# A graph network's count matrix: own products in fp32, evicted behind the third eviction of counts

## The reference

```python
def _layer(x, rows, cols, vals, W, b):
    neigh = segment_sum(vals[:, None] * x[cols], rows, num_segments=N)
    cat = concatenate([x, neigh], axis=1)
    return relu(cat @ W.T + b)
x0 = _layer(_layer(x, src, dst, 1/deg, W0, b0), src, dst, 1/deg, W1, b1)
x = layernorm(x + x0)
h_neigh = x @ W_neigh
summed = segment_sum(maxk(h_neigh, 32)[src], dst, num_segments=n)
x = layernorm(x + x @ W_self + summed / max(deg_in, 1)[:, None])
```

## Time and profile before

| what | us |
|---|---|
| median of the 3 timed runs | 697.11 |
| the three runs | 697.01, 697.11, 700.86 |
| the profiled execution | 701.42 |
| its span, first to last instruction | 699.6 |
| TensorE busy in it | 641.8 |
| VectorE busy | 505.9 |
| ScalarE busy | 348.7 |
| GpSimd busy | 106.9 |

### The profile page before, as it was taken

How to read it: one execution, slowest core, us unless ns; L and a number is a source line. 1 busy time by engine, 2 the same in 40 slices (tenths; PEclk the granted TensorE clock), 3 DMA queues, 4 the chain that set the end, 5 groups by cost and what they waited for, 6 DMA issues and landing times.

```text
span 699.6 us, 11372 instructions
## 1 busy us (share of the span) xinstructions
PE 641.8 (92%) x4012; PEld 338.4 (48%) x4013; DVE 505.9 (72%) x1296; ACT 348.7 (50%) x669; POOL 106.9 (15%) x188
## 2 busy tenths in 40 slices
PE   8867788888787999999999999999999889999996
PEld 3355566666643444444444444444444334444443
DVE  8659989999768788888883578787877844634433
ACT  3588888899847777777774223333333220100000
POOL 3001222222111001010100222323232210000000
PEclk9789999999998999999999999999999999999999
DMA  9423554555531011111111555555656414310000
GB/s 212 91 91 113 188 162 137 162 161 158 157 101 37 29 43 33 41 34 40 36 40 39 156 174 164 172 167 169 176 162 182 121 36 135 115 47 23 22 28 25
DMA packets 39542, 73.08 MB, mean 104 GB/s; under 512 B 3120, under 2 KB 32207, under 8 KB 39481
## 3 DMA queue, kind: packets, MB, share of 16 engines
q1 hardware_dynamic: 39481, 72.30, 34.8%
HBM read 38.91 MB, written 33.38 MB: 103 GB/s over the span
## 4 chain that ended last, share of the span: by engine, by line
PE 72%; DVE 17%; ACT 7%; issue 2%; DMA 2%; POOL 0%; SPq 0%; ACTq 0%; DVEq 0%; POOLq 0%
PE pair L1567 36%; PE bank L1679 9%; PE pair L1679 8%; PE bank L1467 7%; DVE hots L639 6%; PE pair L1467 4%; PE bank L1459 2%; DVE ct L782 2%; ACT own L1128 2%; DVE x_t L775 2%; PE bank L1473 1%; PE pair L1363 1%; DMA own_in<-own_dram 1%; ACT x_t L1121 1%; ACT slab L1078 1%
## 5 line engine op out<-in xcount | busy, mean ns | idle before, releaser
L1567 PE MATMUL pair<-xs,ct 125*128 125x512 f16 x625 | 144.1, 381 | 0.0
L1567 PE MATMUL pair<-a,ct 125*128 125x512 f16 x625 | 142.8, 379 | 0.0
L639 DVE TENSOR_TENSOR hots<-iota,jobs 125x1792 f16<-125x1792 f16 (+1 forms) x100 | 104.5, 1063 | 1.3 <-PE pair L1380 0.7
L1567 PEld LDWEIGHTS pair<-xs,ct 125*128 125x128 f16 x625 | 61.3, 100 | 68.7 <-issue 1.8
L1567 PEld LDWEIGHTS pair<-a,ct 125*128 125x128 f16 x625 | 61.0, 99 | 68.1
L1078 ACT ACTIVATE slab<-pair 125x875 f16<-125x875 f32 (+1 forms) x100 | 83.4, 858 | 5.6 <-PE pair L1380 4.1
L1245 ACT ACTIVATE a<-ct 125x1000 f16<-125x1000 f16 (+1 forms) x75 | 80.2, 1069 | 0.9
L1679 PE MATMUL bank<-xs,ct 125*128 125x512 f16 (+1 forms) x325 | 71.5, 379 | 0.0
L1679 PE MATMUL pair<-xs,ct 125*128 125x512 f16 x300 | 66.4, 379 | 0.0
L1459 PE MATMUL bank<-ident,slab 125*128 125x125 f16 x625 | 52.7, 224 | 14.0 <-DVE ct L782 9.9
L1318 ACT ACTIVATE sd<-mv,epsb 125x1 f32<-125x1 f32 x25 | 7.4, 294 | 113.9 <-DVE mv L998 113.9
(11 more groups left out here) (213 smaller groups left out, 852.9 us busy)
## 6 DMA issues: line engine op xcount, KB each, us to landing
c_dram<-slab SPq DMA_DIRECT2D x25, 683.6 KB
ct<-c_dram SPq DMA_DIRECT2D x25, 683.6 KB
own_in<-own_dram SPq DMA_DIRECT2D x50, 125.0 KB
own_dram<-own SPq DMA_DIRECT2D x25, 125.0 KB
own_dram<-own_st SPq DMA_DIRECT2D x25, 125.0 KB
x_in<-in_x_dram SPq DMA_DIRECT2D x25, 125.0 KB
z_dram<-z_st SPq DMA_DIRECT2D x25, 125.0 KB
a<-z_dram SPq DMA_DIRECT2D x5, 625.0 KB
```

The source lines that it names most:

```text
L639: v.tensor_tensor(hots[k][:, :, :, :].rearrange("p w g (a d) -> p (w g) a d", d=2), iota, job, ALU.is_equal).then_inc(win_hot, 1)
L1567: ins = mm(agg[k % 3][0:lhs.shape[1], :], lhs, parts[l][:, t, :], start=t == 0, stop=t == NT - 1, skip_group_check=True)
```

## The change

- An own product is two fp32 instructions (one per half, 512 columns each) on the fp32 transposed block and the fp32 transposed W0, where it was six fp16 matmuls. `own_low` and the split of W0 are gone: four weight halves are split (tiles 3 and 4), not six.
- The own eviction and the eviction of x_t stand behind ScalarE's third eviction of counts and ahead of its eviction of transposes of group 2; they stood ahead of the third eviction of counts.
- `OWN` starts in tile 3 and takes two products in tiles 8, 13 and 18.
- The statistics: the three squares of x in ScalarE's stream write their sums into `stat`, and a step on VectorE takes the root as a power of two from the bits. The fourth block of x and the weights are bounded by their largest magnitude on VectorE (tile 1). The roots and their table load are gone. The bounds move to tile 2 on TensorE and VectorE.
- In the second set of picks one warm matmul follows each of the 8 groups of three; `KEEP` loses its entry for tile 2.

```diff
-OWN = {0: [], 1: [], 2: [], 3: [], 4: [0], 5: [1], 6: [2], 7: [3, 4], 8: [5], 9: [6, 7], 10: [8], 11: [9, 10], 12: [11],
-       13: [12, 13], **{t: [t] for t in range(14, NT)}}
+TWOS = (8, 13, 18)
+OWN = {t: [] for t in range(3)}
+for _t in range(3, NT):
+    _n = sum(map(len, OWN.values()))
+    OWN[_t] = [_n, _n + 1] if _t in TWOS else [_n]
-KEEP = {0: 4, 1: 2, 2: 1}
+KEEP = {0: 4, 1: 2}
...
+            def largest_x(c):
+                dve.wait_ge(x_loaded[c], BOTH)
+                v.tensor_reduce(stat[0:P, c:c + 1], xs32[:, XC[c]:XC[c + 1], :].rearrange("p t f -> p (t f)"), X, ALU.max,
+                                apply_absolute_value=True).then_inc(stat_ready, 1)
+
+            def largest_w():
+                dve.wait_ge(b_loaded, 16)
+                v.tensor_reduce(stat[:, 14:16], bcol[:, :].rearrange("p (h o) -> p h o", o=1), X, ALU.max,
+                                apply_absolute_value=True).then_inc(stat_ready, 1)
...
+                step(v.tensor_scalar(sv[:, 0, 0:3].bitcast(I32), sv[:, 0, 0:3].bitcast(I32), 0.5, float((127 << 22) + (16 << 23)),
+                                     ALU.mult, ALU.add))
...
-            def own_low(t):
-
-                dve.wait_ge(own_tcopied, t + 1)
-                v.scalar_tensor_tensor(x_t16[:, 2:4, 0:P], xp, scales[:, 0:1], x_t16[:, 0:2, 0:P], ALU.mult, ALU.subtract
-                                       ).then_inc(own_tlo, 1)
...
-                a.activation(x_t16[:, 0:2, 0:P], xp, ACT.Copy, scale=scales[:, 0:1]).then_inc(own_tcopied, 1)
+                a.activation(x_t32[:, :, :], xp, ACT.Copy).then_inc(own_tcopied, 1)
...
                     quick_copy(t, 0)
-                    tr_copy(t - 1, 0)
...
-                        w_high(0)
-                        w_high(1)
+                    tr_copy(t - 1, 0)
+                    quick_copy(t, 1)
+                    if 2 < t < 5:
+                        w_high(2 * t - 6)
+                    quick_copy(t, 2)
                     if own:
                         own_copy(own[0], own[0] % 2, own[0] // 2)
-                    if t == 3:
+                    if t == 2:
                         own_t(0)
                     if own and own[0] + 1 < NT:
                         own_t(own[0] + 1)
-                    quick_copy(t, 2)
                     tr_copy(t - 1, 2)
-                    if t == 1:
-                        roots()
+                    if 2 < t < 5:
+                        w_high(2 * t - 5)
                     quick_copy(t, 3)
...
+                        if k:
+                            keep_clock(bank[7], 1)
                 last.then_inc(picked, 1)
+                if k == 0:
+                    pe.wait_ge(wt_copied, 2)
...
                 if h == 0:
-                    pe.wait_ge(own_tlo, t + 1)
+                    pe.wait_ge(own_tcopied, t + 1)
                     pe.wait_ge(own_copied, t + 1)
-                    pe.wait_ge(w_split, 2)
-                last = in_parts(bank[6][0:P, :], lambda k: x_t16[:, k, 0:P], w0_parts, (h,))
+                    pe.wait_ge(wt_copied, 2)
+                last = mm(bank[6][0:P, :].rearrange("p (a f) -> p a f", a=2), x_t32[:, h, :], w0_t[:, h::2, :], start=h == 0, stop=h == 1,
+                          skip_group_check=True)
...
                     fill(t, 0)
-                    if t == 3:
-                        scales_b()
+                    if t == 2:
+                        bounds_t()
...
                     transposes(t - 1, par, 0)
+                    fill(t, 1)
                     if t == 2:
-                        bounds_t()
-                    fill(t, 1)
+                        bounds_row()
...
                     transposes(t - 1, par, 2)
                     if t == 2:
-                        bounds_row()
+                        scales_b()
```

112 lines of the change are left out of this document (44 added, 68 removed).

## The result

| | before | after |
|---|---|---|
| median of the runs | 697.14 us (697.01, 697.11, 697.18, 700.86) | 709.07 us (706.84, 708.96, 709.17, 709.23) |
| profiled execution, its span | 701.42, 699.6 | 706.84, 705.0 |
| first transposes of tile 3, of tile 24 | 55.28, 186.02 | 54.17, 193.97 |
| first aggregation of the layers | 193.47 | 201.34 |

The ratio of the times is 1.0162, 95% interval 1.0131 to 1.0193: the changed kernel is 12 us slower. The forecast was 701.7 with a range up to 707.0, so it is wrong by 7.4 us and the time lies outside the range.

The account below looks back on a forecast made before the run. The loop through the slab was to replace VectorE as the bound of the count-matrix build. From 697.1: +4.2 stage, +0.7 start, -0.1 last tile, -0.2 picks gives 701.7 us; range 693.5 to 707.0.

Parts of the forecast that it names:

- loop of 5.76: Plain tile of the count-matrix build: loop through the slab takes 5.76 us, against 5.67 before; VectorE and ScalarE have slack.
- own half 0.86: TensorE's fp32 own half of 512 columns, taken as two matmul records of 0.43 us each.
- rival B: Own product: the fp32 half costs 0.43 us, a plain tile 5.33; time 688.4 us; chance 0.12.
- rival D: Plain tiles: links overlap more and a tile runs at VectorE's 5.2 us; time 692.7 us; chance 0.08.
- +0.7: Start of the stage, up to tile 3's transposes: new chain of scales costs +0.7 us, between -1 and +2.5.
- -2.0: Second picks: warm matmuls bring the clock back near 19.5 us; last pick ends near 24.8, 2.0 us earlier.
- Tiles 3 and 4 ... 8.3: Tiles 3 and 4, two weight splits each: VectorE's second split waits for ScalarE's, so 8.3 us a tile.
- Tiles with two own products ... 8.7 a tile: The three double tiles: 1.00 + 1.93 us extra over a plain tile, so 8.7 us each.
- on SP's queue ... I book nothing: SP's queue: slab's store stands behind own's; DMA engines busy 0.52 of a tile, so no cost was booked.
- forecast 134.9: Tile 3's first transposes to tile 24's: 92.2 + 26.1 + 16.6 = 134.9 us, against 130.74 before, so +4.2.
- -0.2: Picks in an ordinary run: -0.2 us, the middle of a 2.0 gain and a 1.7 cost.
- Rival C: Picks: warm matmuls do not bring the clock back, +3.4 instead of -0.2; 705.3 us from the median; chance 0.20.

Follow-up runs that it names:

- run with both moves: Changed kernel with VectorE's second low part of the split weights behind all four hots and the first double tile at 7: 702.63 us, ratio 1.0072.
- run with the late splits alone: Changed kernel with only VectorE's second low part of the split weights in tiles 3 and 4 moved behind the next tile's four hots: 705.83 us.
- 686 us version: Changed kernel with second own half behind the third fill, splits behind the hots and first double tile at 7: 686.07 us, ratio 0.9837 to the kernel before.

## Why the prediction was wrong

**Right: what bounds a plain tile, and by how much.** It was laid out as a loop of 5.76 in place of VectorE's 5.67, and measured 5.73. The terms: own half 0.86, measured 0.91; third fill, 0.54, measured 0.53 (153.02 to 153.55); ScalarE's wait before the third count eviction "some 0.6", measured 0.68. The x_t copy came shorter than taken (0.26 from its start to the next, not 0.35). Tiles 13 and 18 were to take 8.7 and took 8.80. The halves at 0.43 (rival B) and VectorE's tile of 5.2 (rival D) did not come. The Trainium skill ("FP8 and Floating Point Precision", TensorE Precision Notes) counts four passes for true FP32. The trace agrees: 0.91 is 4.2 times the 0.217 that an fp16 matmul of 512 columns took here (three in 0.65), and 256 columns took 0.48.

**Right by chance in the profiled pair, wrong as a term: the start.** Tile 3's transposes were to start 1.3 earlier in the profiled pair (+0.7 and -2.0), and started 1.1 earlier. The picks gave -3.6 rather than -2.0, so the rest was +2.5, the end of the range given for it. And it is no chance of one execution: the profiles with the old scales and with the new ones do not overlap there (27.55 to 28.44 against 29.89 to 31.35 us). In the medians, where the picks give nothing, nothing hides it, and the +0.7 was 1.8 too small. The condition that the prediction named for the upper end held: TensorE, which had stood twice, went at 1.2 GHz there, and the first own half, booked at 0.86, took 1.84 (52.33 to 54.17):

```profile
52.33 2.04 PE L1479 MATMUL bank<-w_t,x_t 128*125 128x512 f32 x2 [0.82 <-issue]
```

**Wrong: "Tiles 3 and 4 ... 8.3".** Tile 3 took 8.43, near the forecast in part because one of its own halves ran at half clock (56.16, 2.02 in the records); in the profile without the warm matmuls it took 7.48. Tile 4 took 9.67, and tile 5, counted as plain, 7.53 instead of 5.76: together 3.1 too little. Two things were left out of the working. The sum of 8.4 was made from one set of eight transposes to the next, at full clock; TensorE, standing behind VectorE, fell to 0.50, and an own half of 0.91 took 1.81 (65.57 to 67.38; 2.02 against 1.08 in the records). With the clock at 1.00 the same tile took 8.14, so this is 1.5 of the 3.1. And a time from eight transposes to eight was put into a sum from five to five: in tile 5 the eight start 2.44 behind the five (74.71 and 72.27), in a plain tile 0.62, and the 1.8 between the two falls to tile 5, which took 7.54 in the profile without the warm matmuls, too. Moving the splits gave back 3.2 of the 12 us.

**Wrong: "Tiles with two own products ... 8.7 a tile", for tile 8.** It took 10.71. The prediction looked at the number of double tiles, three instead of four, and not at what stood where. The double tile 7 had been the cover of the weights' store; the term "on SP's queue ... I book nothing" is the step that failed. It named the stores of the slab and of own, and left out the one that a later tile waits for. Moving the double tile back gave 3.6. The 2.0 are the price at full clock; where the clock fell behind the wait, tile 8 took 13.29 and 13.64. Whether it did so in the other three executions of the changed kernel, 2.1 to 2.4 us longer than the profiled one, is not shown: their mean clocks are 0.977 and 0.978, as in the profiled one.

So in the profiled pair, from tile 3 to tile 24: forecast 134.9, measured 139.8; of the 4.9 missing, 3.1 lie in tiles 4 and 5, 2.0 in tile 8, 0.3 in tiles 3, 13 and 18, and the plain tiles gave 0.5 back. If the pair's stage and start stand for the medians too, then of the 7.4 us the stage is 4.9, the start 1.8 and the picks 0.2; the 0.5 left is within what two medians can differ by. The run with both moves gives back 6.4, more than the 5.1 of the two places, since it also makes tiles 3 and 4 shorter than the forecast had them (7.80 and 6.41).

**The picks, rightly at nothing.** The median basis booked -0.2, and the two runs say 0. The reason given, that the ordinary runs of before already had a better clock there, is borne out as far as it can be: the same code shows both clocks from one profile to another. Of the executions that were not profiled only the mean granted clock is on record, and it fits: of 55 executions of the kernel before in the four comparisons the 11 above 700 us had 0.975 to 0.980, the 18 below 697 us 0.979 to 0.990. So the long ones have a lower clock on the whole, as the prediction read the 700.86. Where in the execution it was lower a mean can't tell. Rival C, half clock all the way with the warm matmuls in, came in no profile.

**The step not taken.** The prediction found that the changed tile would be bound by a loop with slack on all three engines, and stopped there. Its own links name the cure: 0.86 + 0.22 of own work between the eight transposes and the third fill, none of which the slab needs. With these behind the fill the tile is 4.92, TensorE and VectorE full. The prediction put VectorE's tile at 5.2, from a busy time of 5.61 less 0.4, and even that was too long: its largest hot takes 1155 ns on average in the kernel before (100 to 170 us), 1391 in the changed one and 1075 with the half behind the fill. Why is not shown.

## What to carry to other kernels

Where an edit takes work off the fullest engine, lay out the loop that closes through the others and look for operations on it that nothing in the loop needs; moving these was worth more (15.8 us) than the whole change had at stake. Ask of every tile that becomes shorter or moves what it had covered, transfers with a deadline above all: two such places, worth 3.2 and 3.6 us on the medians, were most of the miss here. And when a wait moves into one tile, count it from the same mark to the same mark, follow its delay into the next tile, and price TensorE's work behind it at the lower clock too. One profile shows one of the two prices: tile 8 of the same code took 10.71 and 13.29.

## What was not expected of the hardware

- The granted clock at the same dense stretch of matmuls (16 to 26 us) was 1.00 in eight and 0.50 at first in four profiles of kernels with the warm matmuls there; without the warm matmuls it stayed at 0.50 past 24 us in two of three. The row eviction behind this stretch came anywhere from 23.2 to 26.9 us. In the kernel before the clock had been 1.00 up to 16 us and fell as the dense stretch began; TensorE's last long stand before that was 1.14 us, up to 13.75. The Trainium skill ("TensorE: Matmul & The Clock Gate", the HAM clock gate) says that activity releases the throttle, and that the moment varies from run to run; the spread agrees, while 9.8 us of busy TensorE at 0.50 goes beyond what it leads one to expect.
- Waits can bring the clock down, and the fall costs a second time: an fp32 own half of 1.08 in the records took 2.02 behind the waits in tile 4, and again at 95.58 in the run with the late splits alone. It does not come in every execution. Behind TensorE's waits of 0.78 and 1.65 in tile 4 the clock fell in the changed kernel's profile and stayed at 1.00 in the one without the warm matmuls; behind the waits of 1.27 and 1.71 in tile 8 it was the other way round.
- In the tightest tiles ScalarE's operations became longer. A count eviction had a median of 842 ns in the changed kernel and 957 in the 686 us version (between 100 and 170 us in both), of the same shapes:

```profile
L1068 ACT ACTIVATE slab<-pair x43: 810/842/963, 101.0 to 168.1; 125x750 f16<-125x750 f32 x32, 125x875 f16<-125x875 f32 x11
```

```profile
L1068 ACT ACTIVATE slab<-pair x53: 811/957/1059, 100.1 to 169.9; 125x750 f16<-125x750 f32 x40, 125x875 f16<-125x875 f32 x13
```

  The shortest is the same, 810 and 811. What lengthens the others (a shared memory, or a start in the queue that the record counts in) no run here tells. Nor is a full engine enough: with ScalarE's own eviction ahead of the third count eviction it worked 5.04 of a tile's 5.27, and the median was 840. VectorE's largest hot went the other way, 1391 ns on average in the changed kernel and 1076 in the 686 us version. A duration from a loose profile can thus be wrong for a tight one in either direction.
